# Normed cross attention in a decoder kernel: one product for keys and values, four heads' squares together, context split a stage earlier, inputs in two loads

## The reference, cut to what matters

```
q = rmsnorm(layernorm(x) @ Wq.T)   per head of 128 channels, 32 heads, times q_norm_w
k = rmsnorm(ctx @ Wk.T)            per head of 128 channels,  8 heads, times k_norm_w
v = ctx @ Wv.T                     8 heads
p = softmax(q @ k.T / sqrt(128) + mask)      within each sequence of 64 tokens
x = x + concat(p @ v) @ Wo.T
```

## Time and profile before

| what | value |
|---|---|
| time, median of 3 runs | 2727.82 us (2726.18 to 2729.58) |
| time of the profiled execution | 2728.66 us |
| its span, first to last instruction | 2726.5 us |
| mean granted TensorE clock | 0.951 |
| busy: PE, DVE, ACT, POOL | 88%, 53%, 39%, 24% |
| transfers issued for the stage's weights | 17 of 1024 KB (query), 16 of 1024 KB (output), 9 of 512 KB (values), 17 of 256 KB (keys) |

### The profile page before, as it was taken

The page is one execution under the profiler, slowest core; times in us unless marked ns, Lnnn a source line. Parts: engine busy times, 40 slices in busy tenths (PEclk is TensorE's granted clock), DMA queues, the critical chain, the costliest instruction groups (busy, mean ns, idle before and its releaser), DMA issues. The chain is left out here.

```text
span 2726.5 us, 45735 instructions
## 1 busy us (share of the span) xinstructions
PE 2409.6 (88%) x18034; PEld 1892.1 (69%) x18034; DVE 1432.4 (53%) x2391; ACT 1058.5 (39%) x1682; POOL 650.8 (24%) x434
## 2 busy tenths in 40 slices
PE   4998499999999799999999769999969996899787
PEld 3676377777777577777777557877857774677576
DVE  4666444343434544343434546867745554565555
ACT  4554244444444444444434421011135433554322
POOL 0000223232222423222212341211232223333200
PEclk9999699999999899999999879999979998899978
DMA  3000201011101201110110120000010001000001
GB/s 105 2 1 2 75 28 38 33 43 36 42 18 36 74 20 43 36 43 17 36 44 35 66 88 1 0 0 0 0 54 1 2 1 71 17 17 1 7 20 62
DMA packets 25066, 82.95 MB, mean 30 GB/s; under 512 B 3504, under 2 KB 5808, under 8 KB 19632
## 3 DMA queue, kind: packets, MB, share of 16 engines
q1 hardware_dynamic: 24880, 80.16, 8.5%
HBM read 75.96 MB, written 4.19 MB: 29 GB/s over the span
## 5 line engine op out<-in xcount | busy, mean ns | idle before, releaser
L103 PE MATMUL xat_TP<-xat_Wo,xat_oT_hi 128*128 128x512 f32 x1024 | 323.0, 396 | 19.8 <-DVE xat_oT_lo L1982 11.8
L1948 DVE RECIPROCAL xat_k_rms<-xat_k_rms 128x512 f32<-128x512 f32 x32 | 107.3, 3353 | 355.2 <-ACT xat_k_rms L1805 355.2
L103 PE MATMUL xat_G<-xat_xnT_hi,xat_Wq 128*128 128x512 f32 x768 | 277.0, 421 | 0.0
L103 PEld LDWEIGHTS xat_TP<-xat_Wo,xat_oT_hi 128*128 128x128 f32 x1024 | 187.3, 188 | 74.3 <-issue 23.5
L1881 POOL TENSOR_TENSOR xat_T<-xat_T,xat_mask 128x512 f32<-128x512 f32 x64 | 81.9, 1290 | 601.9 <-DVE xat_T L1963 601.9
L103 PE MATMUL xat_TP<-xat_Wo,xat_oT_lo 128*128 128x512 f32 x512 | 199.9, 390 | 0.0
L1990 DVE TENSOR_TENSOR X<-X,xat_TP 128x512 f32 x128 | 86.9, 679 | 184.7 <-PE xat_TP L103 184.7
L103 PEld LDWEIGHTS xat_G<-xat_xnT_hi,xat_Wq 128*128 128x128 f32 x768 | 144.2, 188 | 50.4 <-issue 20.4
L103 PE MATMUL ffn_H<-ffn_w,ffn_xnT_hi 128*128 128x448 f32 x512 | 149.3, 373 | 25.0 <-DVE ffn_h_kept L1060 25.0
L985 ACT ACTIVATE ffn_hT_hi<-ffn_TP 128x384 fp32r<-128x384 f32 x64 | 34.9, 545 | 312.8 <-PE ffn_Y L1106 256.6
L103 PE MATMUL xat_G<-xat_xnT_lo,xat_Wq 128*128 128x512 f32 x384 | 151.5, 395 | 0.0
(11 more groups left out here) (411 smaller groups left out, 5945.8 us busy)
## 6 DMA issues: line engine op xcount, KB each, us to landing
xat_weights_raw<-in_Cq_q SPq DMA_DIRECT2D x17, 1024.0 KB, 6.7
xat_weights_raw<-in_Cq_o SPq DMA_DIRECT2D x16, 1024.0 KB, 5.0
xat_weights_raw<-in_Cq_v SPq DMA_DIRECT2D x9, 512.0 KB, 3.9
xat_weights_raw<-in_Cq_k SPq DMA_DIRECT2D x17, 256.0 KB, 2.7
X<-in_x SPq DMA_DIRECT2D x1, 4096.0 KB, 13.4
xat_qT<-in_ctxT_paired SPq DMA_DIRECT2D x4, 1024.0 KB, 6.6
cga_ctxT_raw<-in_ctxT SPq DMA_DIRECT2D x4, 1024.0 KB, 5.5
out<-X SPq DMA_DIRECT2D x4, 1024.0 KB, 4.3
```

Of the source, the lines that this page charges most:

```text
L103: last = eng.matmul(out, a, b, start=(n == 0), stop=(n == len(steps) - 1))
L1948: chain(eng.reciprocal(krms[:, :], krms[:, :]))
```

## The change

1. `load_constants` loads only the first 512 tokens of `X`; the other 1536 are loaded from inside the next block, behind four weight and scale loads, under a semaphore that DVE waits for before the second stage's statistics.
2. `small_attention` of kind "sign" also loads the first half's context and the first pair's key and value weights into its own raw rooms, and splits them in twelve pieces of 128 by 512, one at the end of each of the steps 16 to 27 (ACT rounds, POOL subtracts). `sum_o` and `ysc` share the room of other tiles for it.
3. Keys and values of both groups of a pair come from one product: context across the partitions, 512 columns of weights stream past (`kv_product`, eight of 12 matmuls into eight uses of banks). ACT copies keys and values apart, DVE squares and sums the keys (`square_k`) and scales them by the inverse root (`norm_k`, now 8 numbers per stage), PE turns them (`turn_k`, 16 transpositions per pair), and ACT copies them to `kT` with the norm weights. The product with ones is gone.
4. The four heads of a stage are projected one after the other, and the sums of their squares are taken together after them. `squares` has four buffers.
5. The norm of `X` at a half's start is laid between the pair's key and value products, in banks of its own (`x_turn`, lists `AFTER` and `LATE`).
6. The second half's context is loaded and split in the two groups of the last pair of the first half.
7. Weights: one room for query and output, one for keys with values; the 128x2048 key and value weights are rounded by ACT between `exponent(2)` and `exponent(3)` of `gg` 0 and subtracted by POOL between `bias(3)` and `normalize(2)`.
8. DVE's order after `invert_q(1)` changes: both `low_oT` come before `shift(2)`.
9. The loops over halves and pairs are written out in full.

```diff
+            ysc = sum_q
             sum_k = mem.sb("k_abs_sum", [P, P])
             sum_v = mem.sb("v_abs_sum", [P, P])
-            sum_o = mem.sb("o_abs_sum", [P, D])
+            sum_o = rk[:, :, :].rearrange("p k n -> p (k n)")
+            early_of = [(early[0][:, k, st * STOK:(st + 1) * STOK], early[1][:, k, st * STOK:(st + 1) * STOK], raw[:, k, :])
+                        for st, raw in ((0, rq), (1, ro)) for k in range(KC)]
+            early_of += [(early[2][0][:, k, :], early[2][1][:, k, :], rq[:, k, :]) for k in range(KC)]
+            EARLY = {2 * NP + n: n for n in range(3 * KC)}
...
+                load_x(eng, X, dram["x"], 1, NST).then_inc(x_rest.sem, 16)
             eng.dma_start(PK(ro), dram["o"]).then_inc(w_landed[3].sem, 16)
+            if sign:
+                eng.wait_ge(w_sum.sem, w_sum.at(0, 4))
+                for st, dst in ((0, rq), (1, ro)):
+                    eng.dma_start(dst[:, :, :], dram["next_ctxT"][:, :, st * STOK:(st + 1) * STOK])\
+                       .then_inc(e_landed.sem, 16)
+                eng.wait_ge(e_lo.sem, e_lo.at(0, KC))
+                eng.dma_start(rq[:, :, :].rearrange("p k n -> p (k n)"), dram["next_kv"][:, 0:KC * D])\
+                   .then_inc(e_landed.sem, 16)
...
+                if sign and s in EARLY:
+                    n = EARLY[s]
+                    eng.wait_ge(e_landed.sem, e_landed.at(0, 32 if n < 2 * KC else 48))
+                    eng.activation(early_of[n][0], early_of[n][2], ACT.Copy).then_inc(e_hi.sem, 1)
...
+                for n in range(3 * KC):
+                    eng.wait_ge(e_hi.sem, e_hi.at(0, n + 1))
+                    hi, lo, raw = early_of[n]
+                    eng.tensor_tensor(lo, raw, hi.bitcast(F32), ALU.subtract).then_inc(e_lo.sem, 1)
...
+    AFTER = {2: (0, 0), 3: (0, 1), 4: (0, 2), 5: (0, 3), 6: (1, 0), 7: (1, 1)}
+    LATE = ((1, 2), (1, 3))
...
-        VB = [S[0], S[1], G[1], S[0]]
...
+        KB = [S[0], S[1], G[0], G[1], OT[0], OT[1], S[0], S[1]]
+        XB = {(0, 0): TP[0], (0, 1): TP[1], (0, 2): TP[0], (0, 3): TP[1],
+              (1, 0): TP[0], (1, 1): TP[1], (1, 2): OT[0], (1, 3): OT[1]}
+        TB = [[S[0], S[1]], [OT[0], TP[1]]]
...
+            for j in range(PASSES):
+                g = j % NG
+                jp, gg = divmod(j, 2)
+                eng.wait_ge(wq_lo.sem, wq_lo.at(j, 1))
+                load(raw, a["Cq_o"], g, wo_landed)
+                if jp == PAIRS - 1:
+                    eng.wait_ge(wkv_lo.sem, wkv_lo.at(jp, gg))
+                    load_context(gg)
+                elif gg == 0 and jp + 1 < PASSES // 2:
+                    eng.wait_ge(wkv_lo.sem, wkv_lo.before(jp))
+                    load(raw_kv, a["Cq_kv"], (jp + 1) % PAIRS, wkv_landed)
...
+            def keep_kv(jp, m):
+                eng.wait_ge(kv_done.sem, kv_done.at(jp, m + 1))
+                eng.activation(Kn[:, 2 * m:2 * m + 2, :], KB[m][:, 0:2 * P].rearrange("p (g d) -> p g d", g=2),
+                               ACT.Copy).then_inc(kr_ready.sem, 1)
+                eng.activation(V[:, m, :], KB[m][:, 2 * P:], ACT.Copy).then_inc(v_ready.sem, 1)
...
+                if gg == 0 and jp + 1 < PASSES // 2:
+                    eng.wait_ge(wkv_landed.sem, wkv_landed.at(jp, 16))
+                    eng.activation(Wkv[0][:, :, :], raw_kv[:, :, :], ACT.Copy).then_inc(wkv_hi.sem, 1)
+                exponent(3)
...
+                bias(0)
+                bias(1)
+                normalize(0)
+                normalize(1)
+                eng.wait_ge(wo_hi.sem, wo_hi.at(j, 1))
+                low(Wo, raw).then_inc(wo_lo.sem, 1)
+                if jp == PAIRS - 1:
+                    eng.wait_ge(ctx_hi.sem, ctx_hi.at(0, gg + 1))
+                    eng.tensor_tensor(cl[:, :, half_of(gg)], raw_kv[:, :, :],
+                                      ch[:, :, half_of(gg)].bitcast(F32), ALU.subtract).then_inc(ctx_lo.sem, 1)
+                bias(2)
+                bias(3)
+                if gg == 0 and jp + 1 < PASSES // 2:
+                    eng.wait_ge(wkv_hi.sem, wkv_hi.at(jp, 1))
+                    low(Wkv, raw_kv).then_inc(wkv_lo.sem, 1)
+                normalize(2)
+                normalize(3)
+                if j + 1 < PASSES:
+                    low_wq(j + 1)
...
+            def square_k(jp, m):
+                junk = PT[:, m % 2, 0:2, :]
+                eng.wait_ge(kr_ready.sem, kr_ready.at(jp, m + 1))
+                eng.tensor_tensor(junk, Kn[:, 2 * m:2 * m + 2, :], Kn[:, 2 * m:2 * m + 2, :], ALU.mult)\
+                   .then_inc(k_squared.sem, 1)
+                eng.wait_ge(k_squared.sem, k_squared.at(jp, m + 1))
+                eng.reduce_sum(ksum[:, 2 * m:2 * m + 2], junk, AX_X).then_inc(k_summed.sem, 1)
+
+            def norm_k(jp, st):
+                at = slice(st * KV, (st + 1) * KV)
+                eng.wait_ge(krms_ready.sem, krms_ready.at(jp, st + 1))
+                eng.reciprocal(kinv[:, at], krms[:, at]).then_inc(k_inverse.sem, 1)
+                eng.wait_ge(k_inverse.sem, k_inverse.at(jp, st + 1))
+                eng.tensor_tensor(Kn[:, at, :], Kn[:, at, :], kinv[:, at].unsqueeze(2).to_broadcast([P, KV, P]),
+                                  ALU.mult).then_inc(kn_ready.sem, 1)
...
-                        norm_k(1)
-                        invert_q(1)
-                        take_scores(2)
-                        low_oT(1)
-                        take_scores(3)
-                        shift(2)
-                        low_oT(0)
-                        shift(3)
...
+                invert_q(1)
+                low_oT(1)
+                take_scores(2)
+                low_oT(0)
+                take_scores(3)
+                shift(2)
+                shift(3)
...
+            def kv_product(jp, m):
+                if m >= 6:
+                    eng.wait_ge(v_ready.sem, v_ready.at(jp, m - 5))
+                at = slice(m * P, (m + 1) * P)
+                products(eng, KB[m][:, :], [((ch[:, k, at], cl[:, k, at]), (Wkv[0][:, k, :], Wkv[1][:, k, :]))
+                                            for k in range(KC)]).then_inc(kv_done.sem, 1)
+
+            def turn_k(jp, st):
+                eng.wait_ge(kn_ready.sem, kn_ready.at(jp, st + 1))
+                eng.wait_ge(v_ready.sem, v_ready.at(jp, KV))
+                for g in range(2):
+                    for q in range(ST):
+                        last = eng.transpose(TB[st][g][:, q * P:(q + 1) * P], Kn[:, 2 * (st * ST + q) + g, :],
+                                             ident[:, :])
+                    last.then_inc(kt_done.sem, 1)
...
-                            eng.matmul(OT[0][:, :], ones[:, :], sq[:, (st * (1 + NH)) % 2, :], start=True, stop=True)\
-                               .then_inc(ms_done.sem, 1)
-                            head(1)
-                            q_squares(0)
-                            head(2)
-                            q_squares(1)
-                            head(3)
-                            q_squares(2)
-                            if st == 1:
-                                turn_probs(0)
-                                turn_probs(1)
-                                q_squares(3)
-                                scores(2)
-                                turn_rms(1)
-                                values(1)
-                                scores(3)
-                                values(0)
-                            else:
-                                scores(0)
-                                q_squares(3)
-                                scores(1)
...
+                        last = eng.matmul(OT[1][t * QC:(t + 1) * QC, 0:P], sel[:, NH - 1 - h:NH - 1 - h + QC],
+                                          sq[:, h, t * P:(t + 1) * P], start=(h == 0), stop=(h == NH - 1),
+                                          tile_position=(0, t * QC))
+                    last.then_inc(ms_done.sem, 1)
...
+                eng.wait_ge(ol_ready.sem, ol_ready.before(j))
+                if gg == 0:
+                    eng.wait_ge(s_read.sem, s_read.before(j))
+                    eng.wait_ge(pt_ready.sem, pt_ready.before(j))
+                    eng.wait_ge(wkv_lo.sem, wkv_lo.before(jp))
+                    if g == 0:
+                        eng.wait_ge(ctx_lo.sem, ctx_lo.at(0, 2 * hf))
+                        eng.wait_ge(y_added.sem, y_added.before(j))
+                    for m in range(KV):
+                        kv_product(jp, m)
+                        if g == 0 and m in AFTER:
+                            x_turn(hf, *AFTER[m])
+                    if g == 0:
+                        for st, t in LATE:
+                            x_turn(hf, st, t)
+                        eng.wait_ge(ln.hi_ready.sem, ln.hi_ready.before(hf * 2 + 1))
+                        eng.wait_ge(ln.lo_ready.sem, ln.lo_ready.at(hf * 2 + 1, 1))
+                if j == 0:
+                    eng.wait_ge(small.sem, small.at(0, 16 * 4))
```

(40 more changed lines are left out.)

879 lines of the change are left out of this document (410 added, 469 removed).

## The result

The changed kernel takes 2656.26 us in the median of 4 runs (2653.94 to 2658.01), the kernel before 2727.0 us beside it: ratio 0.974, 95% interval 0.9723 to 0.9757. That is 70.7 us less; 52.9 were forecast, and 2656.26 lies inside the range of 2652 to 2694. The profiled execution has a span of 2656.2 us against 2726.5, so 70.3 less.

What follows compares the result with a forecast made beforehand. PE's own sequence was taken to bound the pair loop, with PE idle where halves begin and at the start. From the profiled 2728.7 us, -8.0 + 2.5 - 34.1 - 17.8 + 4.5 = -52.9 gave 2675.8, 2675 against the median; range 2652 to 2694.

Steps and rivals of the forecast that it cites:

- start: Program start: with a smaller first load the second block begins near 8 instead of 15.8, 8 us less.
- first seam: Start of the cross attention: 39.7 us before its first product go, 5.6 return for turns of X, net 34.1 less.
- second seam: Start of the second half: 21.4 us idle and 2.9 slow clock and wait go, 5.6 and 0.9 come, 17.8 less.
- pairs: All eight pairs: seven that load weights lose 5.6 us together, the eighth gains 3.1; with late context 4.5 lost.
- case c: Rival at the program start: POOL, not the load, holds the first block; 8 us more, 2683; chance 0.09.
- The early pieces: First self attention: ACT's 12 more copies cost 2.5 us, between 0 and 7.
- Ports: First seam: norm of X on DVE overlapping POOL's query-weight subtraction would cost up to 4.2 us once, giving 2679; not summed.
- What a pair saves: Steady pair: ones product, switches, scores' wait, loop's turn and wider products save 7.3 us; after costs 3.1 shorter.
- The new wait: gg 0 of seven loading pairs: POOL's 4.61 us subtraction delays normalizing, fourth output product 4.35 late, pair 0.8 longer.
- case (d): Rival in the pairs: POOL's wait is smaller than counted, or switches gain more; 2645 to 2655; chance 0.11.
- case (f): Rival in stage 0: its chain is no longer covered and the kernel is slower, 2733 at 15 us; chance 0.02.
- Case (b): Rival in seven groups: the clock falls behind PE's wait, about 2 us each, 14 more, 2689; chance 0.18.

Runs made afterwards that it cites:

- The experiment's order: Squares between heads again in 30 of 32 stages, on the changed kernel with weights split later, DVE's old order, spread increments, earlier query-weight rounding: 2639.32 us.
- the run with two places: Changed kernel with the first block's 113 semaphore increments shared by POOL, ACT and DVE, and first query weights rounded two products earlier: 2649.68 us.
- its split: The kernel before with only the inputs loaded in two parts, nothing else of the change: 2719.6 us, ratio 0.998.

## Why the prediction was right, and where its sizes were off

The mechanism and the direction were right; the likeliest case was 18.7 us too high. That the result lies inside the range is in part luck: an error in the clock and errors in the savings went opposite ways (below). By its own terms, from the two profiles:

| term | forecast | profiles |
|---|---|---|
| start | -8.0 | -5.6 |
| first self attention | +2.5 | -3.9 (of it 5.2 chance in the profile of before) |
| first seam | -34.1 | -33.8 |
| second seam | -17.8 | -20.1 |
| pairs | +4.5 | -10.4 |
| later blocks | 0 | +3.5 |
| sum | -52.9 | -70.3 |

How they are counted: pairs 2, 3, 6 and 7 differ from before by -0.84, -0.96, +0.28 and -1.21, and pair 4 by +0.31, of which 0.87 is the wait for the last sum before the second half and stands with that seam; in the mean -0.66. Seven times that and the last pair's -5.79 make -10.4. What pairs 1 and 5 differ by beyond -0.66 stands with the seams: the first is 38.75 less between the last product of the block before and the first of this one (44.65, now 5.90) and 4.9 more in pair 1; the second is 21.5 less, 0.5 more in pair 5 and the 0.87.

**The start** was held by POOL (case c), in a milder form: 10.2, and the increments are 113 instead of 103. 2.4 of the forecast 8 us did not come, and the experiment that spread the increments gave 3.1 us: there the block begins at 7.1, when the last load has landed, and this part of the prediction's reasoning (near 8) was sound.

**The early pieces** cost 0 to 0.9 us, not 2.5. ACT had room for them in its steps.

**First seam**: the sum was right, its parts were not. The gaps closed as forecast. A turn of `X` costs 0.35 for the transpositions and 0.1 for the product behind it, not 0.7, and two behind one another 0.79, so eight cost 3.7 and not 5.6; two things that the sum did not have came in their place, the slow clock of the first products (7.04 us for 24 matmuls that take 5.44 at the full clock) and the stall of 2.29. That the sum still comes out is because the kernel before had a slow start too: its first pair took 152.2 us against 149.0 for the second, and the forecast counted such a loss (2.9 us) only for the second seam. The second seam now has neither, and of the 2.3 us that it gained beyond the forecast the cheap turns are 1.9.

**Ports.** The prediction put an overlap of POOL's subtraction with the norm of `X` at up to 4.2 us and summed without it. It came, once, through the scaling of the keys: 3.94 us instead of 1.23, and 2.29 on PE's path. The Trainium skill (SBUF — State Buffer, Who interferes with whom) has the pair of ports as an exclusive lock for the whole instruction, also against a VectorE operation with two inputs in SBUF. The traces agree with the lock: both delayed operations ended behind POOL's. They agree also that operations that read PSUM are left alone: the low part of `X` at 295.08 took its 0.69.

**What a pair saves** was the step that failed most, by size. The last pair, where no load stands in the way, saves 5.8 us; forecast were 3.1. The price of the squares was read from one transition: 0.19 per switch, 8 switches, 1.5 us, and 1.3 for the scores' wait. But it is three of four heads in each of four stages, 12 switches, and squares behind one another take 0.25 each and not 0.35: these two and the wait are 4.2 by the experiment instead of 2.8. The experiment's order is near that of the kernel before and not the same: its scores wait 0.33, there it was 0.67. Keys and values take 21.8 us against 22.8 (four key products of 2.72 to 2.86 and the values' 11.5): 1.0, not 0.3. `turn_k` costs 1.6 and some 0.1 on the heads behind it, not 2.4. The wait for the last sum was right (0.87), and so, nearly, was the order's 0.45 as a difference to the kernel before (0.89 against 0.49), though not as the price of the order: 0.95.

**The new wait** came nearly to the tenth. Counted from the turn of the norms at 636.01: rounding at +8.6 (+8.7 forecast), POOL's subtraction from +10.6 to +15.1 (+10.6 to +15.2), the fourth output product at +17.6 (+17.8). Over the seven groups this product starts at +17.6 to +18.0. The half of case (d) that had this wait smaller is out; its other half, more gained at the switches, came true with the forecast. The 2 us set down for the context in the fourth pair did not come: with the wait of 0.87 taken off, that pair is like the others.

The price of the new wait was right as well: the two pairs of the run with two places in which the clock stayed up are 3.9 us longer than those without the wait (147.1 and 147.0 against 143.2), and 3.9 is what the prediction has. Stage 0's chain stayed covered: PE waits in no group in front of `turn_probs(0)`. The sum in case (f) is some 3 us low: 15 us less the 11.2 of four heads is 3.8, and 16 times that on 2675 is 2736, not 2733. Nothing else rests on it.

**The clock.** Case (b) had 0.18 and was true: behind each of the seven waits of 3.1 us the granted clock was 0.52 to 0.73 in the next 6 us. The row that I leaned on the earlier trace rows was one instance of 2.90 us, and I read it over too short a stretch. Its eight transpositions ran at the high clock, but the clock fell 1.1 us behind the wait; the window of 6 us from 2643.96 in the kernel before:

```profile
2643.96:2649.96 6.00, 6.00 (x23) 4.79 (x24) 4.95 (x13) 1.49 (x3) 0.00 (x0) 0.72 0.01 3
```

So the row spoke for case (b), and its chance of 0.18 was too low. In the changed kernel the fall cost 1.1 to 2.2 us per group, near the 2 forecast. So a loaded pair lost 4.9 to 6.1 us to its wait and the clock (148.1 to 149.3 against 143.2), where the sum had 3.9, and this nearly ate the 5.8.

**The later blocks** were taken at nothing and gave back 3.5. Their code and order are the same. The lead is 73.8 us where the cross attention ends, wanders between 67.2 and 75.6 along them, and loses most at the beginning of the second cross attention (names beginning with cga), where the clock is 0.73 (2206 to 2256 us) against 0.83 in the kernel before (2280 to 2330). From the start of the cross attention's last output matmul to the end, the same code took 1176.5 to 1179.3 us in the three profiles of the kernel before and its split, and 1177.0 to 1184.4 in the nine of the changed kernel and the runs on it (1182.2 in its own). So 3.5 us lies within what this code varies by from one execution to the next.

So two errors stood against one another: the clock, some 10 us against the kernel over the seven groups, and the savings, 2.7 us in each of eight pairs for it. The start, the pieces and the turns stand beside them.

## What to carry to other kernels

Large work on a side engine belongs behind the small operations that the bottleneck waits for, even when its own result is not late: here its place decided 37 us, as much as the whole first seam was worth, and moving two steps got it back. When a change takes an operation off an engine, look again at what it delayed by the shared ports or by its place; an order that was right before may now be the wait. Price a repeated pattern from the whole stretch (four heads and their squares) and not from one transition times a count, and profile the same kernel twice before a few microseconds in an untouched part are explained. When a row is to show that the clock did not fall behind a wait, read the granted clock over several microseconds behind it.
